# Attention probabilities turned by VectorE and outputs from V by token, in a six-layer stream

## The reference, cut to what matters

```python
q, k, v = split(x @ Wqkv)                 # by head; q and k normalized, rotary tables applied
bk2, bv2 = look(bk), look(bv)             # keys, values of the window before and of its own: 64
sim = einsum('bhwie,bhwje->bhwij', bq, bk2) * QK_SCALE     # QK_SCALE = 8
attn = softmax(where(mask, -max, sim), -1)
out = einsum('bhwij,bhwje->bhwie', attn, bv2)
x = x + out.transpose(0, 2, 1, 3).reshape(b, n, INNER) @ Wo
x = x + (a * gelu(gate)) @ W2 + b2        # a, gate = split(layernorm(x) @ W1 + b1)
```

## Time and profile before

| | |
|---|---|
| median of 3 runs | 1991.57 us |
| the profiled execution's own time | 1989.8 us |
| its span, first to last instruction | 1988.0 us |
| mean granted TensorE clock | 0.962 of full speed |
| busy: PE, PEld | 1813.1 us (91%), 1253.7 us (63%) |
| busy: DVE, ACT, POOL | 1488.6 (75%), 1241.9 (62%), 1233.2 us (62%) |
| DMA packets | 89905, 137.49 MB |

### The profile page before, as it was taken

How to read it: one execution, slowest core, us unless ns; L and a number is a source line. 1 busy time by engine, 2 the same in 40 slices (tenths; PEclk the granted TensorE clock), 3 DMA queues, 4 the chain that set the end, 5 groups by cost and what they waited for, 6 DMA issues and landing times. The chain is left out here.

```text
span 1988.0 us, 75625 instructions
## 1 busy us (share of the span) xinstructions
PE 1813.1 (91%) x31926; PEld 1253.7 (63%) x31926; DVE 1488.6 (75%) x2834; ACT 1241.9 (62%) x2410; POOL 1233.2 (62%) x789
## 2 busy tenths in 40 slices
PE   8487873899999999999999999999999999999984
PEld 2154452467766667776776767676767677767662
DVE  6699844777877777878777777787777778777743
ACT  6523212567676767676767676767676767676751
POOL 3467731876666666766666666666666666666630
PEclk9799966999999999999999999999999999999996
DMA  4434003223222242232333222422224323222220
GB/s 99 56 38 69 1 3 138 67 66 73 61 70 60 70 117 71 63 72 60 109 80 75 61 70 62 122 64 71 65 70 116 74 60 76 62 69 61 70 53 21
DMA packets 89905, 137.49 MB, mean 69 GB/s; under 512 B 27296, under 2 KB 32864, under 8 KB 88544
## 3 DMA queue, kind: packets, MB, share of 16 engines
q1 hardware_dynamic: 89568, 132.66, 27.9%
HBM read 29.80 MB, written 2.10 MB: 16 GB/s over the span
## 5 line engine op out<-in xcount | busy, mean ns | idle before, releaser
L1269 POOL TENSOR_TENSOR qk<-qk,rnorm 128x1024 f32<-128x1024 f32 x192 | 361.2, 1902 | 366.1 <-ACT rnorm L1494 361.2
L1263 POOL TENSOR_TENSOR qk<-qk,turnedhalf 128x1024 f32<-128x1024 f32 x192 | 454.5, 2367 | 138.3 <-DVE turnedhalf L1620 138.3
L1616 DVE TENSOR_TENSOR qk<-bank,gains 128x512 f32<-128x512 f32 x384 | 263.2, 685 | 236.9 <-ACT squares L1484 225.2
L1320 PE MATMUL bank<-wqkv,x 128*128 128x512 f32 x768 | 378.9, 597 | 24.5 <-DMA qk_gain<-in_qk_gain 22.5
L1484 ACT ACTIVATE squares<-bank 128x512 f32<-128x512 f32 x384 | 232.9, 607 | 166.5 <-PE bank L1320 165.0
L1620 DVE TENSOR_TENSOR turnedhalf<-bank,gains 128x256 f32<-128x256 f32 x768 | 286.8, 416 | 0.0
L1531 ACT ACTIVATE o_T<-bank 128x512 f32<-128x512 f32 x192 | 104.2, 598 | 228.9 <-PE bank L1384 228.6
L1626 DVE TENSOR_REDUCE rnorm<-squares 128x16 f32<-128x1024 f32 x192 | 230.9, 1203 | 2.8
L1384 PEld LDWEIGHTS bank<-p_T,v_win 64*64 64x64 f32 x12288 | 189.3, 135 | 59.6 <-issue 58.2
L1333 PEld LDWEIGHTS bank<-st_ident,qk 128*128 128x128 f32 x1536 | 176.6, 141 | 56.9 <-issue 50.8
L1325 PE MATMUL bank<-wqkv,x 128*128 128x512 f32 x384 | 202.8, 610 | 4.5 <-DVE turnedhalf L1620 4.4
(11 more groups left out here) (199 smaller groups left out, 2951.5 us busy)
## 6 DMA issues: line engine op xcount, KB each, us to landing
v_win<-v_tok SPq DMA_DIRECT2D x1536, 64.0 KB
wqkv<-in_wqkv SPq DMA_DIRECT2D x6, 1536.0 KB
v_rep_sb<-v_by_step SPq DMA_DIRECT2D x32, 128.0 KB
v_rep<-v_by_step SPq DMA_DIRECT2D x32, 128.0 KB
wo<-in_wo SPq DMA_DIRECT2D x6, 512.0 KB
w<-in_w SPq DMA_DIRECT2D x6, 341.0 KB
w<-in_w SPq DMA_DIRECT2D x6, 192.0 KB
xT_sb<-in_xT SPq DMA_DIRECT2D x1, 1024.0 KB, 4.7
```

What stands on the lines that cost most here:

```text
L1263: nc.gpsimd.tensor_tensor(out=qk[n % 2][:, half], in0=qk[n % 2][:, half], in1=turnedhalf[:, half], op=ALU.add).then_inc(rot_added.sem, 1)
L1269: nc.gpsimd.tensor_tensor(out=by_head(qk[u][:, half]), in0=by_head(qk[u][:, half]), in1=rnorm[u][:, AH * i:AH * (i + 1)].unsqueeze(2).to_b ...
L1320: nc.tensor.matmul(QK_BANKS[i][:, :], shifted_tokens(x, n, P), layer_cols(wqkv, n, 3 * INNER, 512 * i, 512), start=True, stop=True).then_i ...
L1616: nc.vector.tensor_tensor(by_head(qk[u][:, cols]), src, cos.to_broadcast([P, 8, DH]), ALU.mult).then_inc(rotated.sem, 1)
```

## The change

- `turn_p` is no longer TensorE's. VectorE turns the probabilities in one instruction, in squares of 32 by 32 (`nc.vector.transpose`), from `probs` straight into `p_T`: the 32 tokens of a window are one square's rows, the 32 keys of one half (window before, own window) its columns. `p_T` now has the keys of one half on the window's 32 partitions. It stands between `rotate` 1 and `peaks` in VectorE's list. ScalarE's `read_p` is gone.
- `outputs` takes V by token. The weights are 32 tokens by 128 channels (a pair of heads), from `v_prev` for the half before and from `v_tok` for the own half; the moving data are 32 keys by 64 columns (two heads of 32 tokens). Each product runs in one of four row tiles of 32x128, window w in row tile w and in bank 4 + w, and the two halves are summed in PSUM. Of the 128x64 result only the half that belongs to the right head is read.
- `v_prev` is `v_tok` moved on by 32 tokens, filled by two DMAs a block instead of 16. `v_tok` has four buffers instead of three and keeps its natural column order; Wo's rows are ordered to match.
- `read_o` reads eight pieces (window by head) of 64 partitions x 256.
- Order at the start of a turn. TensorE: project V 1, gate tail, project QK 0, turn Q, turn K (before: project V 1, turn K, gate tail, turn Q, project QK 0). Both turnings now wait until `read_o` has emptied their banks. ScalarE: read V 1, gelu tail, square 0, read Q, read K (before: read K, gelu tail, read Q, read V 1, square 0).

```diff
-V_SLOTS = 3
+V_SLOTS = 4
...
-        v_win = two("v_win", (P, WINDOWS, INNER // 2))
-        probs, p_T = two("probs", (P, PAIRS, 2, DH)), sb("p_T", (P, PAIRS, P))
+        v_prev = two("v_prev", (P, INNER))
+        probs, p_T = two("probs", (P, PAIRS, 2, DH)), sb("p_T", (P, PAIRS, 2, 2, WINDOW))
...
-        v_placed = sig("v_placed", per=16 * 16)
+        v_placed = sig("v_placed", per=2 * 16)
+        total_made, p_normed, pT_made = sig("total_made", per=2), sig("p_normed"), sig("pT_made")
+        o_product, oT_made = sig("st_o_product", credit=V_SLOTS), sig("oT_made", per=2 * WINDOWS)
...
+        O_BANKS = S_BANKS + T_BANKS
...
                 sp.wait_ge(v_read.sem, v_read.after(n))
                 sp.wait_ge(o_product.sem, o_product.after(n - 2))
                 sp.wait_ge(v_placed.sem, v_placed.after(n - 1))
-                for p in range(2):
-                    cols = slice(p * INNER // 2, (p + 1) * INNER // 2)
-                    for w in range(WINDOWS):
-                        own, before = slice(WINDOW * w, WINDOW * (w + 1)), slice(WINDOW * (w - 1), WINDOW * w)
-                        sp.dma_start(v_win[u][DH * p + WINDOW:DH * (p + 1), w, :], tok[own, cols]).then_inc(v_placed.sem, 16)
-                        src = tok[before, cols] if w else last[P - WINDOW:P, cols]
-                        sp.dma_start(v_win[u][DH * p:DH * p + WINDOW, w, :], src).then_inc(v_placed.sem, 16)
+                sp.dma_start(v_prev[u][WINDOW:P, :], tok[0:P - WINDOW, :]).then_inc(v_placed.sem, 16)
+                sp.dma_start(v_prev[u][0:WINDOW, :], last[P - WINDOW:P, :]).then_inc(v_placed.sem, 16)
...
-            def transposes(outs, turned, source, read, n):
+            def transposes(outs, turned, source, n, first):
 
                 for i in range(PAIRS):
                     if i % 4 == 0:
-                        pe.wait_ge(read.sem, read.after(n, i // 4 + 1))
+                        pe.wait_ge(oT_made.sem, oT_made.after(n - 2, 2 * (first + i // 4 + 1)))
                     mm = nc.tensor.transpose(outs[i // 4][:, P * (i % 4):P * (i % 4 + 1)], source[:, P * i:P * (i + 1)], ident[:, :])
                     if i % 4 == 3:
                         mm.then_inc(turned.sem, 1)
 
             def turn_q(n):
                 pe.wait_ge(qk_made.sem, qk_made.after(n, 1))
-                transposes(S_BANKS, q_turned, qk[n % 2][:, 0:INNER], oT_made, n - 2)
+                transposes(S_BANKS, q_turned, qk[n % 2][:, 0:INNER], n, 0)
 
             def turn_k(n):
                 pe.wait_ge(qk_made.sem, qk_made.after(n, 2))
-                transposes(T_BANKS, k_turned, qk[n % 2][:, INNER:2 * INNER], pT_made, n - 2)
+                transposes(T_BANKS, k_turned, qk[n % 2][:, INNER:2 * INNER], n, 2)
...
                     mm.then_inc(s_product.sem, 1)
 
-            def turn_p(n):
-                pe.wait_ge(p_normed.sem, p_normed.after(n))
-                transposes(T_BANKS, p_turned, probs[n % 2][:, :, :, :].rearrange("p a b d -> p (a b d)"), kT_made, min(n + 1, STREAM - 1))
-
             def outputs(n, q):
 
                 if q == 0:
                     pe.wait_ge(pT_made.sem, pT_made.after(n))
                     pe.wait_ge(shifted.sem, shifted.after(min(n + 1, STREAM - 1)))
+                    pe.wait_ge(kT_made.sem, kT_made.after(min(n + 1, STREAM - 1)))
                     pe.wait_ge(v_placed.sem, v_placed.after(n))
-                for w in range(WINDOWS):
-                    for side in range(2):
-                        for p in range(2):
-                            a_, at, rows = 2 * q + side, WINDOW * w, slice(DH * p, DH * (p + 1))
-                            mm = nc.tensor.matmul(S_BANKS[p][DH * side:DH * (side + 1), P * q + at:P * q + at + WINDOW],
-                                                  v_win[n % 2][rows, w, DH * a_:DH * (a_ + 1)], p_T[rows, a_, at:at + WINDOW],
-                                                  start=True, stop=True, skip_group_check=True)
+                for a_ in (2 * q, 2 * q + 1):
+                    for half, v in enumerate((v_prev[n % 2], v_tok[n % V_SLOTS])):
+                        for w in range(WINDOWS):
+                            rows = slice(WINDOW * w, WINDOW * (w + 1))
+                            mm = nc.tensor.matmul(O_BANKS[w][:, DH * a_:DH * (a_ + 1)], v[rows, P * a_:P * (a_ + 1)],
+                                                  p_T[rows, a_, half, :, :].rearrange("k p t -> k (p t)"),
+                                                  start=(half == 0), stop=(half == 1), skip_group_check=True)
                 if q == QUARTERS - 1:
                     mm.then_inc(o_product.sem, 1)
...
             def turn(at, pair):
                 at(1, project_v, 1)
+                pair(6, up_gate_tail)
+                at(0, project_qk, 0)
+                at(2, turn_q)
                 at(2, turn_k)
-                pair(6, up_gate_tail)
-                at(2, turn_q)
-                at(0, project_qk, 0)
                 pair(6, up_a_full)
                 pair(5, variances)
                 at(0, project_qk, 1)
@@ -1453,7 +1446,6 @@
                 at(2, scores, 1)
                 at(2, scores, 2)
                 at(2, scores, 3)
-                at(3, turn_p)
...
             def read_v(n, i):
                 act.wait_ge(v_placed.sem, v_placed.after(n - V_SLOTS + 1))
+                act.wait_ge(o_product.sem, o_product.after(n - V_SLOTS))
                 act.wait_ge(v_product.sem, v_product.after(n, i + 1))
-                out = v_tok[n % V_SLOTS][:, :].rearrange("p (b a d) -> p b a d", b=2, d=DH)[:, :, 4 * i:4 * i + 4, :]
-                nc.scalar.activation(out, V_BANKS[i][:, :].rearrange("p (a b d) -> p b a d", b=2, d=DH), ACT.Copy).then_inc(v_read.sem, 1)
+                nc.scalar.activation(v_tok[n % V_SLOTS][:, 512 * i:512 * (i + 1)], V_BANKS[i][:, :], ACT.Copy).then_inc(v_read.sem, 1)
...
-            def read_p(n):
-                act.wait_ge(o_product.sem, o_product.after(n - 1))
-                for i in range(2):
-                    act.wait_ge(p_turned.sem, p_turned.after(n, i + 1))
-                    nc.scalar.activation(p_T[:, 4 * i:4 * i + 4, :].rearrange("p a t -> p (a t)"), T_BANKS[i][:, :], ACT.Copy).then_inc(pT_made.sem, 1)
-
             def read_o(n):
                 act.wait_ge(y_product.sem, y_product.after(n // PAIR - 1))
                 act.wait_ge(o_product.sem, o_product.after(n))
-                at = P * (n % PAIR)
-                for p in range(2):
-                    nc.scalar.activation(o_T[:, 4 * p:4 * p + 4, at:at + P], S_BANKS[p][:, :].rearrange("p (q t) -> p q t", t=P),
-                                         ACT.Copy).then_inc(oT_made.sem, 1)
+                for w in range(WINDOWS):
+                    at = P * (n % PAIR) + WINDOW * w
+                    for p in range(2):
+                        rows = slice(DH * p, DH * (p + 1))
+                        nc.scalar.activation(o_T[rows, :, at:at + WINDOW], O_BANKS[w][rows, :].rearrange("d (a p t) -> d a p t", p=2, t=WINDOW)[:, :, p, :],
+                                             ACT.Copy).then_inc(oT_made.sem, 1)
...
             def turn(at, pair):
+                at(1, read_v, 1)
+                pair(6, gelu_tail)
+                at(0, square, 0)
+                at(2, read_q)
                 at(2, read_k)
-                pair(6, gelu_tail)
-                at(2, read_q)
-                at(1, read_v, 1)
-                at(0, square, 0)
                 pair(5, inverse_sigma)
                 pair(6, logs_and_exps)
                 at(0, square, 1)
                 at(1, inverse_norms)
                 pair(5, affine)
-                at(3, read_p)
                 at(0, square, 2)
                 at(0, square, 3)
...
             def shifts(n):
-                dve.wait_ge(p_turned.sem, p_turned.after(n - 2))
+                dve.wait_ge(pT_made.sem, pT_made.after(n - 2))
...
+
+            def turn_p(n):
+                dve.wait_ge(p_normed.sem, p_normed.after(n))
+                dve.wait_ge(o_product.sem, o_product.after(n - 1))
+                nc.vector.transpose(p_T[:, :, :, :, :].rearrange("k a h p t -> k a p h t"),
+                                    probs[n % 2][:, :, :, :].rearrange("t a p (h k) -> t a p h k", h=2)).then_inc(pT_made.sem, 1)
...
                 pair(6, gated_tail)
                 at(0, rotate, 1)
+                at(3, turn_p)
                 at(2, peaks)
                 at(2, shifts)
                 pair(6, add_ffn)
...
-    wo = asn("Wo").reshape(DEPTH, PAIRS // 2, 2, 2, DH, C).transpose(0, 2, 4, 3, 1, 5)
+    wo = asn("Wo").reshape(DEPTH, PAIRS, 2, DH, C).transpose(0, 2, 3, 1, 4)
```

8 lines of the change are left out of this document (3 added, 5 removed).

## The result

The changed kernel takes 2331.73 us (median of four runs, 2328.98 to 2333.66). The kernel before, run beside it, takes 1992.69. The ratio is 1.169, 95% interval 1.165 to 1.173: 339 us slower. The forecast was 2227 us with a range up to 2300. The direction is as forecast and the size lies beyond the range; of the mechanism the odd turn is as forecast, the even turn only in part.

A forecast was written before the change was run, and what follows sets the result against it. TensorE bounds the kernel, with thin slack on the others. Even turn 16.5 plus odd turn 21.4 give 37.9 us a pair against 32.96: +4.94 x 48, less 2 at the ends, +235, so 2227 us; range 2110 to 2300, chance 0.80.

The forecast's parts named there:

- the odd turn: The turn with the output projection: add_ffn ends at 14.1, output projection starts at 14.15, turn 21.4 us against 18.79.
- the even turn: The turn without the output projection: 16.5 us, against 13.87 without the pause.
- The even turn's path: Turn without output projection: square 1, rotate 1, transpose, peaks and shifts end at 12.7; outputs wait, TensorE idle 1.9 us.
- Outputs: TensorE's output products: weight loads of 128 columns make a group 112 ns for 59, 1.7 us more a turn.
- B (first form): Outputs on TensorE keep 59 ns a group, 34.5 us a pair, 2066 us; chance 0.09 for both forms.
- C: Loads and matmuls of a row tile in series, 165 ns, 41.3 us a pair, 2390 us; chance 0.05.
- D: Outputs stay at 59 ns and VectorE's transpose fits into time it has: -90 us, 1902 us; chance 0.04.
- B's second form: The chain ScalarE to VectorE hides and TensorE's own 34.5 us a pair stands, 2066 us; chance 0.09 for both forms.
- E: TensorE's new idle stretches bring its clock down to 1.2 GHz in places, beyond 2300 us; chance 0.02.
- The transpose: On VectorE between rotate 1 and peaks: one instruction of 1.22 us (1.05 to 1.67), delaying peaks and shifts.
- The DMAs: Sixteen transfers of 64 KB a block become two: put at nothing, at most a gain of 0.3 us a pair.
- The copies: ScalarE's read_o: eight copies overlapping by 0.11 take 2.39 us, 1.30 more; without overlap 3.1, with no fixed part 1.09.

The follow-up runs named there:

- experiment 2: Changed kernel with VectorE's transpose of the probabilities moved to the head of its turn: 2279.51 us, ratio 1.140 to the kernel before.
- Experiment 11: Changed kernel with 32 moving columns instead of 64 in each output product, right heads' outputs left out: 2358.49 us, ratio 1.180 to the kernel before.
- Experiment 5: Changed kernel with four 128x256 copies in read_o (right heads left out) and the transpose at the head of VectorE's turn: 2092.43 us, ratio 1.047.
- experiments 9 to 12: Changed kernel with 32x64 head tiles and four copies: 2434.95 us; early transpose besides: 2352.11; also 64 moving columns: 2309.65; row tiles with 32 moving columns: 2358.49.
- experiment 4: Changed kernel with read_o as four copies of 128x256, right heads' outputs left out: 2149.12 us, ratio 1.076 to the kernel before.
- experiment 3: Changed kernel with read_o's eight copies ordered by head, four of partitions 0 to 63, then four of 64 to 127: 2258.47 us, ratio 1.130.
- experiment 10: Changed kernel with outputs in eight 32x64 head tiles, four copies, and the transpose at the head of VectorE's turn: 2352.11 us, ratio 1.178.

## Why the prediction was wrong

**What bounds it: right.** TensorE's slack was as thin as the earlier trace rows said; it now stands idle before the scores, before up_gate and before the output projection, as the prediction named, and at gate_T, which it did not name.

**The even turn's path: wrong.** The prediction said of the shifts' end at 12.7 "The outputs wait for that". They don't: with the shifts 1.1 us earlier the turn kept its length (experiment 2). TensorE's idle time in it, 2.06 us against the 1.9 forecast, is all for q_T, k_T and xn_T, which ScalarE writes, and the last of these waits sets the turn. That path happens to be as long as the forecast one through the shifts, so the length of the turn was near for a reason that the prediction did not give; this is luck. The transpose costs time in the odd turn alone.

**Outputs: right.** 3.73 us from the first of them to the centres (forecast 3.7 and 3.8), four tiles in 112 ns. Experiment 11 shows why: the loads set the rate. Of the two rules of "TensorE: Matmul & The Clock Gate" of the Trainium skill that the prediction set against each other, the section LDWEIGHTS stands (columns count), and Part 3's span of packed tiles, which leaves loads out, does not hold where each tile loads its own weights: it would shorten the stage with half the moving columns, and 3.53 became 3.50 us. Experiment 5 bears out the sum made of it: 34.75 us a pair less 0.6 of waits for xn_T, against 34.5 with all pauses of the kernel before in it (34.2 without). Rivals B (first form), C and D fall with it; B's second form falls with the waits. E stayed out of this kernel but for some 10 us, and came with half the moving columns and with the head tiles (experiments 9 to 12).

**The transpose: right in size,** 1.235 us for 1.22, and in the chain of the odd turn. Its place is worth 52 to 57 us (experiments 2, and 4 to 5). The DMAs, put at nothing: no wait of TensorE is for v_prev.

**The copies: this is the step that failed.** The prediction said: "they overlap by 0.11, and eight of the new ones take 7 x 0.28 + 0.39 = 2.39 us". They take 3.20, because each starts on another half of the partitions than the last, and then there is no overlap (experiment 3). The overlap was read off two copies that both start on partition 0 and carried to copies that don't. The 0.81 us stand in both turns, unhidden (taking them out shortened the even turn by 0.79 and the odd by 0.80 us, experiment 3), and show in all the places after them:

```
us from the turn's start       forecast   measured
even: square 1 ends                7.73       8.52
      transpose ends              10.25      11.06
      shifts end                  12.7       13.43
      turn ends                   16.5       17.26
odd:  square 1 ends                8.23       9.20
      transpose ends              10.75      11.74
      add_ffn ends                14.1       15.01
      output projection starts    14.15      15.16
      turn ends                   21.4       22.51
```

2 x 0.81 x 48 = 78 of the 105 us that the forecast fell short. The rest is 0.25 us a pair, 12 us, nearly all in the odd turn, in three steps of 0.10: up to the end of add_ffn, from there to the output projection (0.15 us where the forecast had 0.05), and in projection and outputs (7.35 us for 7.25). TensorE's new wait for ScalarE's gelu in that turn (0.75 us for gate_T, L1545) is not among them, as the rows read: TensorE's wait for add_ffn behind it comes last, and VectorE, which needs that product, afterwards still waits 0.62 us for the second square. It was not tested by itself. The last 14 us lie in how the pairs were counted and at the stream's ends, put at -2: the first centring comes 8.3 us later, and the last of the 47 steps takes 35.0 us (2256.0 to 2291.0) where it took 19.9 (1929.5 to 1949.4). The forecast also set a steady pair, read off the time line, against a mean of 46 steps with the stream's longer ones in it (32.96, where the median step is 32.68).

**The range: wrong in its making.** It held the case without overlap (3.1 us, +67 us) and ended at 2300, less than 10 us above it, so any second small error fell outside. Its two upper bounds, +67 and +43, don't give "together 2300": 2227 + 110 is 2337, which would have held 2331.73, though by luck, since the transpose kept to its row. A bound that one row decides, and that was read off a different form, deserved its own share of the chances.

**The split of the cost: too small for ScalarE.** The prediction gave 3.4 of 4.9 us a pair to the weight loads. Measured from below: with four copies and the early transpose the change costs 94 us; the transpose's place adds 57; eight copies in place of four (of half the outputs' columns, experiment 4) add 183; that is 334 of the 339, the rest being within the difference of the chips. More than half of the 339 us is ScalarE copying the outputs in eighths.

## What to carry to other kernels

Where one engine is late by a microsecond only, count what a change puts on the others in sequence, copy by copy, and take the spacing of back-to-back instructions from rows whose start partitions follow each other as the new ones will. A layout that saves TensorE eight transposes and forces its output out in half-partition pieces pays for them on ScalarE. In row tiles, moving data shorter than the weights' columns gained nothing: a group costs its loads.

## What the runs showed of the hardware

- ScalarE's copies out of PSUM overlap by about 100 ns when each works on the same half of the partitions as the last, and not at all when they alternate between the halves (some 271 against 402 ns from start to start, 64x256).
- Row tiles of 32x128 cost 111 to 112 ns a group of four with 64 and with 32 moving columns; eight tiles of 32x64 cost 79 ns where the stage holds no pause, and with 64 moving columns 2.73 us a stage for 2.52.
- With 32x64 tiles, or 32 moving columns in row tiles, TensorE's clock fell to 1.2 GHz within or right behind the outputs in many turns (mean 0.91 to 0.94 in the stream). With 64 moving columns in row tiles it stayed at 1.00.
- With 32x64 tiles TensorE also paused inside nearly every output stage, some 1.9 us, for nothing that the trace shows (149.8 us of 1600 in experiment 10). Pauses and clock together cost more than the smaller work saved.
- A pause in the weight loads alone is not yet a wait: 0.76 us behind a product of 512 columns stood there whether the work it might have waited for ended 0.10, 1.23 or 2.3 us earlier.
